# A selective-scan and FFN block: the loop over chunks with a body of four chunks instead of two

## What is computed

```
xz = x @ W_xproj.T                      # 64 columns dt_raw, 16 columns B, 16 columns C
dt = softplus(dt_raw @ W_dt.T + b_dt)   # (token, 256)
h[t] = exp(dt[t] * -exp(A_log)) * h[t-1] + dt[t] * B[t] * x[t]     # 16 states per channel
y[t] = sum over the states of h[t] * C[t]
x1 = layernorm(x + y + Dp * x)
out = layernorm(x1 + (silu(x1 @ wg.T) * (x1 @ wu.T)) @ wd.T)       # hidden size 768
```

## Time and profile before

| What | Value |
|---|---|
| Median of the runs | 1969.84 us (1969.46 to 1972.84, 3 runs) |
| The profiled execution's own time | 1960.77 us |
| Its span, first to last instruction | 1959.0 us |
| Mean granted TensorE clock | 0.971 |
| TensorE matmul busy | 1718.3 us, 88% |
| TensorE weight load busy | 1365.7 us, 70% |
| VectorE busy | 1715.7 us, 88% |
| ScalarE busy | 1585.7 us, 81% |
| GpSimd busy | 1640.9 us, 84% |
| DMA queue of the kernel's transfers | 214.39 MB, 33.4% of 16 engines |
| Queues of kind "instruction" | q14: 146 packets, 1.20 MB; q8: 17 packets, 0.28 MB |

### The profile page before, as it was taken

One profiled execution on the slowest core, in us unless ns is written; L12 is line 12 of the kernel. 1 busy time (PEld: TensorE's weight loads), 2 busy tenths in 40 slices (PEclk: granted clock), 3 DMA queues, 4 the chain that ended last, 5 costly groups with the idle time before them and its releaser, 6 DMA issues. The chain is left out here.

```text
span 1959.0 us, 37122 instructions
## 1 busy us (share of the span) xinstructions
PE 1718.3 (88%) x11048; PEld 1365.7 (70%) x11048; DVE 1715.7 (88%) x2060; ACT 1585.7 (81%) x2992; POOL 1640.9 (84%) x710
## 2 busy tenths in 40 slices
PE   6789898988898988989888989888989888999977
PEld 4677777776677776777666777776777766777765
DVE  5898999899898888898899898888989899999993
ACT  5778888788888888888888787889888888888863
POOL 6988888888888988888888888988989888889860
PEclk7899999999999999999999999999999999999999
DMA  7322343232443222443233433223433223433200
GB/s 249 108 90 75 137 136 125 92 100 91 136 136 126 93 89 101 136 132 129 78 94 112 136 130 120 87 79 127 136 129 122 86 80 128 136 128 111 76 12 22
DMA packets 107413, 215.87 MB, mean 110 GB/s; under 512 B 10129, under 2 KB 44530, under 8 KB 107250
## 3 DMA queue, kind: packets, MB, share of 16 engines
q1 hardware_dynamic: 107250, 214.39, 33.4%
HBM read 195.48 MB, written 18.87 MB: 109 GB/s over the span
## 5 line engine op out<-in xcount | busy, mean ns | idle before, releaser
L409 POOL TENSOR_TENSOR h<-h,c_bc 128x1024 f32<-128x1024 f32 x352 | 830.5, 2368 | 144.4 <-ACT h_carry L491 81.2
L399 POOL TENSOR_TENSOR ub<-u,b_bc 128x1024 f32<-128x1024 f32 x320 | 754.0, 2371 | 0.1
L923 PE MATMUL p_y<-ident,h 128*128 128x128 f32 x4096 | 531.1, 280 | 27.3 <-POOL h L409 26.0
L505 ACT ACTIVATE p_da<-dt,neg_a 128x512 f32<-128x512 f32 x640 | 434.1, 682 | 134.0 <-DVE h L700 131.6
L923 PEld LDWEIGHTS p_y<-ident,h 128*128 128x128 f32 x4096 | 481.0, 145 | 74.2 <-POOL h L409 34.8
L700 DVE TENSOR_TENSOR_SCAN h<-p_da,ub 128x512 f32<-128x512 f32 x320 | 375.5, 1206 | 50.9 <-ACT p_da L505 30.6
L700 DVE TENSOR_TENSOR_SCAN h<-p_da,h_carry,ub 128x512 f32<-128x512 f32 x320 | 394.1, 1265 | 22.7 <-ACT p_da L505 22.7
L519 ACT ACTIVATE ub_t<-u_t,bc_t 128x256 f32<-128x256 f32 x768 | 344.2, 495 | 29.7 <-issue 29.7
L978 PE MATMUL p_o<-wt_down,hid 128*128 128x256 f32 x1536 | 342.5, 379 | 2.4 <-DVE res L741 1.6
L978 PEld LDWEIGHTS p_o<-wt_down,hid 128*128 128x128 f32 x1536 | 289.0, 190 | 54.6 <-issue 14.7
L897 PE MATMUL p_da<-ident,ub_t 128*128 128x128 f32 x1536 | 241.8, 281 | 34.9 <-DVE h L700 33.2
(11 more groups left out here) (91 smaller groups left out, 1650.3 us busy)
## 6 DMA issues: line engine op xcount, KB each, us to landing
c_bc<-bc_rows_dram SPq DMA_DIRECT2D x352, 256.0 KB, 6.3
b_bc<-bc_rows_dram SPq DMA_DIRECT2D x64, 768.0 KB, 6.3
b_bc<-bc_rows_dram SPq DMA_DIRECT2D x64, 512.0 KB, 3.6
x_in<-in_L_attn_x SPq DMA_DIRECT2D x32, 512.0 KB, 5.8
out_x<-res_n SPq DMA_DIRECT2D x32, 512.0 KB, 3.4
bc_rows_dram<-bc_rows SPq DMA_DIRECT2D x32, 64.0 KB, 1.6
hid<-in_L_ffn_w_gate SPq DMA_DIRECT2D x1, 768.0 KB, 4.9
hid<-in_L_ffn_w_up SPq DMA_DIRECT2D x1, 768.0 KB, 6.7
```

What stands on the lines that cost most here:

```text
L399: nc.gpsimd.tensor_tensor(ub[:, i % UB_SLOTS, :, :], u[:, par, :, :], b_bc[:, i:i + 1, :].broadcast_to([P, DH, T]), ALU.mult).then_inc(s_u ...
L409: nc.gpsimd.tensor_tensor(h[:, s % H_SLOTS, :, :], h[:, s % H_SLOTS, :, :], c_bc[:, i:i + 1, :].broadcast_to([P, DH, T]), ALU.mult).then_i ...
L505: nc.scalar.activation(da, dt[:, par, q, :], ACT.Exp, scale=neg_a[:, q, s:s + 1]).then_inc(done, 1)
L923: ins = nc.tensor.matmul(p_y_tok[:, k, q * P:(q + 1) * P], h[:, s % H_SLOTS, q, k * P:(k + 1) * P], ident[:, :], start=(s == SUM_ORDER[0] ...
```

## The change

The loop's body emits the steps of four chunks instead of two. The number of passes falls from 14 to 7, and the number of jumps back from 13 to 6. The steps themselves, their order, their parities and the thresholds of their waits stay the same; `batch`, the third argument, is still the index of the sequence.

```diff
+UNROLL = 4
...
-    assert DH == 2 and SEQ == 2 * T and CHUNKS >= 4 and N == 16 and NH == 6 and R == 64 and R + 2 * BC == P
+    assert DH == 2 and SEQ == 2 * T and CHUNKS >= 4 and (CHUNKS - 4) % UNROLL == 0 and N == 16 and NH == 6 and R == 64 and R + 2 * BC == P
...
         def over_chunks(eng, step, tail):
             step(0, 0, 0, True, True, False, False)
             step(1, 1, 0, True, True, True, False)
-            with eng.Fori(0, CHUNKS // 2 - 2) as i:
-                step(2 * i + 2, 0, i + 1, True, True, True, True)
-                step(2 * i + 3, 1, i + 1, True, True, True, True)
+            with eng.Fori(0, (CHUNKS - 4) // UNROLL) as i:
+                for k in range(UNROLL):
+                    step(UNROLL * i + 2 + k, k % 2, UNROLL // 2 * i + 1 + k // 2, True, True, True, True)
             step(CHUNKS - 2, 0, CHUNKS // 2 - 1, True, True, True, True)
```

## The result

The changed kernel takes 2002.79 us (median of 4 runs, 1997.93 to 2006.56) against 1969.65 us before (4 runs, 1966.91 to 1972.84). The ratio is 1.0166, 95% interval 1.0135 to 1.0198: slower by 33 us. The mean granted TensorE clock fell from 0.971 to 0.956.

What follows compares the result with a forecast made beforehand. No single engine was taken to bound the kernel; work order and waits between engines set the pace. Jumps saved -5.0, stall +11.7 and clock +2.9 gave +9.6 us on the 1969.84 median: 1979 us, range 1964 to 1988.

Steps and rivals of the forecast that it cites:

- TensorE's body is no longer held: TensorE's loop: the doubled body, 180 KB, was assumed to outgrow its instruction store, with 90 KB known to be held.
- The price of TensorE's stall: TensorE at the six remaining jumps: 3.0 us each, making the chain later by 1.95 us, 11.7 us in all.
- The double load: Rival, TensorE behind a jump: both code blocks late, a stall of 4.5 us, 1988 us; chance 0.13.
- VectorE's second idle time of 0.75 us: VectorE after a jump back: a second pause of 0.75 us, cited for the rival of two late blocks on TensorE.
- TensorE's clock: TensorE behind the remaining jumps: half clock after 2 of 6, 2.9 us in all, bounds 0 and 8.6.
- One for one: Chunk behind a jump: any delay of the chain lengthens the chunk equally, 6 x 1.95 = 11.7 us.
- Jumps removed, 7 x 0.72: Seven jumps back become straight transitions like the loop's exit, saving 5.0 us, bounds 0 and 8.6.
- My yardstick, the loop's exit: Odd-to-even transition without a jump at the loop's end: 57.96 us against 58.68 at a jump, difference 0.72 us.
- GpSimd, SyncE, register computations: Longer loop bodies: GpSimd and SyncE stalls and the computing of wait thresholds were each counted as 0 us.

Runs made afterwards that it cites:

- ScalarE and VectorE straight: Kernel before, two chunks a pass, with ScalarE and VectorE written out without a loop, the other engines looping as before: 1935.18 us, ratio 0.9840.

## Why the prediction was wrong

The mechanism, which no row of before showed for TensorE, was right and its sizes were off: 1979 us with 1988 at the top, measured 2002.8.

- *TensorE's body is no longer held.* The rows left this open between 90 and 180 KB, so it was my assumption. It was right: 89 packets on q8, six jumps with pauses, and TensorE alone decides (1956 without, 2011 with nothing else).
- *The price of TensorE's stall.* The failed step. I sized it at 3.0 us, an estimate from ScalarE's 2.28 us; it was 3.1 + 2.4 and their gaps, 5.8 us, because the target lies 12 instructions ahead of a block's end. The double load stood among the rivals with 4.5 us and a chance of 0.13, and I argued that p_c, p_y and `down` would cover it. They can't where the block's end comes before p_y; where the loop's first instruction lies in its block I had not asked. What I named for the rival was no support either: VectorE's second idle time of 0.75 us in the earlier trace rows is a wait for ScalarE (see "ScalarE and VectorE straight").
- *TensorE's clock.* The second term that was too small: taken as 2 of 6 times 1.43 us. I had seen half the clock behind 2.3 us of idleness in the earlier trace rows; no run shows a share of 2 in 6. In the changed kernel, with two pauses, a slow stretch follows each of the six and covers `down` in whole or in part: 2.5 us at the jump shown. Stall and clock together put `x_out` at 16.4 us, not 11.0. Over the six jumps I had 11.7 + 2.9 = 14.6 us where the trace has 43.7; of the missing 29 us some 6 x (5.8 - 3.0) = 17 are the stall and 6 x 2.5 - 2.9 = 12 the clock.
- *One for one.* Right: `x_out` later by 7.3 us (16.36 against 9.08) and the chunk later by 7.3 (66.0 against 58.7).
- *Jumps removed, 7 x 0.72.* Too small by the times, about right by the traces. The run without TensorE's long body gives 12.6 us (7 to 18) for the seven; the chunks in the traces are 0.6 and 0.7 us shorter in the mean. My yardstick, the loop's exit, had a half-clock stretch of its own at 1817.0, which I had not looked for; against an undisturbed transition a jump costs 1.4 us. It was argued that ScalarE's lateness is the cost. At undisturbed jumps it is the larger part, 0.9 of 1.4 us, but VectorE's pause, to which I gave no share, is 0.5.
- *GpSimd, SyncE, register computations.* Counted as nothing. They were not tested one by one, but with TensorE at two chunks all these long bodies together leave a gain, and straight code for TensorE, which drops its register computations, changed nothing that shows (0.9991).

The sum with the measured sizes: TensorE's body alone cost 41.8 us, the other bodies gained 12.6, together 29 us against 33 measured, which is within the intervals. The saving of 5.0 us hardly matters beside the miss at the six jumps.

## What to carry to other kernels

TensorE's instruction queue was silent in a loop of 1490 instructions and carried 112 packets in one of 1700. So read the instruction queues in the profile and see which is silent in the loop before making a body longer, and choose the length engine by engine: four chunks cost 41.8 us on TensorE and gained 12.6 us on the others. If every jump misses, straight code can be the better form, since streaming TensorE's code cost nothing that shows here (ratio 0.9991). Before taking one transition as a yardstick, read its granted clock, which was 0.50 in a stretch behind the exit used here.

## What the runs showed of the hardware

- A jump into code not held kept TensorE's branch for 3.3 to 4.5 us (0.2 us where the code is held). The engine idled 1.6 to 3.4 us for the first block in the loops of four chunks, and 2.4 to 3.2 us again where the block's end lies 4 or 12 instructions behind the target.
- The next block was asked for only after the jump had ended: at the jump shown the branch ended at 1349.54 us and the packet started between 1350.1 and 1350.4. Moving the same loop by 20 instructions gained 25 to 27 us of 2003.
- TensorE held a loop of 1490 instructions (no packet on q8 between 250 and 1780 us) and reloaded one of 1700 (112 packets between 250 and 2100 us). The length it holds was under 1700 here; the runs don't show why.
- Pauses of TensorE can be paid twice. The granted clock fell to about half (0.51 and 0.52 in two stretches behind the one shown) after each of the six double pauses (3.1 + 2.4 us at the one shown, 2.5 us lost) and after four of the six single ones, which were 1.9 to 3.4 us long.
- VectorE and ScalarE, with loops of some 330 instructions, reloaded them in every pass: 129 packets on q14 over 13 passes, and 52 in the same stretch with both engines straight. A jump cost 1.4 us (58.7 against 57.3). Straight code for these two brought the kernel from 1969 to 1935 us.
